# Rows of h stored as f16 pairs, transposed by DMA instead of by TensorE and ScalarE

## The chip, the cores and the metric

The kernel runs on 1 core of a Trainium2 chip (trn2). The metric is the device time of one launch in microseconds (us), the median of the runs; lower is better. PE is TensorE, DVE is VectorE, ACT is ScalarE, POOL is GpSimd and SP is SyncE, which only issues DMAs here.

## The reference

Two layers over x of 16 sequences x 512 positions x 256 features (8192 tokens), all in f32:

```python
# layer 0: causal attention with 16-wide q and k, values are x itself; layernorm; ternary-weight linear
q, k = x @ w_q.T + b_q, x @ w_k.T + b_k
x1 = softmax(where(causal, q @ k.T / 4, -1e4)) @ x          # added to x, normalised
x2 = layernorm(...) ; x2 @ (ternary(weight) * scale).T      # added, normalised
# layer 1: q, k, v = x @ qkv_w; a similarity of q and k per position gives one gate per position
#          (two small convolutions, softmax over the 512 positions); out = gate * v * ch_w @ proj_w
x3 = x2 + out_of_gate ; h = layernorm(x3) * ln_gamma + ln_beta
# experts: router logits h @ router_w.T, the best of 8 experts, plus one shared expert
shared = silu(h @ q(shared_w1).T) @ q(shared_w2).T           # 256 -> 512 -> 256, weights ternary per row
routed = gate * (silu(h @ q(expert_w1[e]).T) @ q(expert_w2[e]).T)   # for the token's expert e
out = layernorm(h + shared + routed)                         # written at the token's own row
```

What matters here is h, the normalised row of 256 numbers of each token. It is wanted in two layouts and twice: with the features on the partitions (transposed) as the operand of the router and of the shared expert, and again, gathered by expert, as the operand of the routed experts. Each time it is a pair of f16 numbers, a high part and a low part, so that four f16 matmuls stand for one in f32.

## The kernel before

The work has two stages that overlap around 500 to 600 us of the profile.

**The front** goes over the 16 sequences ("batches", b), one after the other, with several in flight: attention (proj, score, scoreT, pv), the ternary linear (x1T, ffn), the gate of layer 1 (x2T, dqk, fuse, u, the small ODE steps on DVE), and then for batch b the part that is changed:
`power2` (POOL, L4017) gives 1/sigma; `hn` (ACT, L1701) writes the normalised row to `HN` in f32, four calls of 128 x 256; `hT` (PE, L855) transposes HN into PSUM banks 6 and 7, two calls of four 128 x 128 transposes; `HT_` (ACT, L1712) evicts each bank as the f16 high part and `HTl_` (DVE, L2407) forms the f16 low part, both times scaled by ln_gamma (`gamc`, one number per partition); `logits` (PE, L865) and `up` (PE, L889) read `HT`; `router` and `place` (DVE) choose the expert and the row; `hsc` (POOL, L4043) scatters the rows of HN and `rsc` (POOL, L4052) those of the residual plus shared expert, `R`, by indirect DMA to two tables in HBM, `hrec` and `rrec`, sorted by expert. The token's number stands in the last column of HN (`hid`, L4034).

**The routed groups** take 256 rows of the tables each: w = 0 to 24 are whole groups of one expert, w = 25 to 35 are pairs of half groups of 128 rows, which may belong to two experts. Groups 0 to 13 can start when 12 batches are in the tables, the others after the last batch has been sorted. Per group: `gload` and `rload` (SP) fetch 256 rows of hrec and rrec; `gTr` (PE, L1060) transposes with four 128 x 128 transposes into one PSUM bank; `gT` (ACT, L1814) and `gTl` (DVE, L3045) evict high and low part to `G_T`; `gup` (PE, L1095), `gsilu` (ACT, L1845), `gSh` (ACT, L1859), `gSl` (DVE, L3053), `gdown` (PE, L1112), `gy` and `gx` (DVE, add bias and residual), `gbn` and `gve` (DVE), `gpower` (POOL, L4106), `gnb_` (DVE), `gn` (ACT, L1866), and two `scatter` (POOL, L4113) to the output rows; `gid_` (POOL, L4099) copies the token numbers out of the loaded rows.

The order of every engine is written out by hand, call by call: each engine is a list of such calls, with loops over pairs of batches (`for g in range(...)`) and over the groups from w = 18 on. An engine takes its list in order, so a call that waits holds up all behind it; SP too, whose list holds the loads of x and xT, of the expert weights, the small `maxima` DMAs (L493, the row maxima of the scores laid into one row, for which `scoreT` waits), and the group loads. Every call opens with its semaphore waits.

## Time and profile before

| | us |
|---|---|
| median of 3 runs (lowest, highest) | 792.61 (790.55, 793.23) |
| span of the profiled execution, first to last instruction | 794.0 |

| engine | busy us | share of the span | instructions |
|---|---|---|---|
| PE | 721.3 | 91% | 5417 |
| DVE | 699.8 | 88% | 2124 |
| ACT | 656.5 | 83% | 1447 |
| POOL | 335.0 | 42% | 370 |

No other time is given for the profiled execution than its span, so the span stands for its own time; it is 1.4 us above the median of the runs. Busy is the time in which an engine has at least one instruction under way, shared out among those that overlap, so the busy time of a group divided by its count is what one of them takes of the engine; its "mean ns" is from start to end and longer. The mean granted TensorE clock is 0.975 of full speed. Of the span, the front holds the first 550 us, with PE busy in nearly all of it; in the rest no engine is busy throughout.

### The profile page before, as it was taken

How to read it: one execution, taken by the hardware profiler on the slowest of the kernel's cores; microseconds unless marked ns; L12 is line 12 of the kernel's file. 1: busy time of each engine (PE TensorE's matmuls, PEld its weight loads, DVE VectorE, ACT ScalarE, POOL GpSimd, SP SyncE). 2: the span in 40 equal slices, each digit the busy share in tenths (PEclk: the TensorE clock that was granted, in tenths of full speed). 3: DMA queues.
4: the chain of work that ended last, by engine and by line, in shares of the span. 5: the costliest groups of instructions: out<-in, count | busy, mean ns of one | idle time of the engine just before them, and what ended most of it. 6: DMA issues, size and time to landing. Idle time of an engine off the chain costs nothing.

```text
span 794.0 us, 18530 instructions
## 1 busy us (share of the span) xinstructions
PE 721.3 (91%) x5417; PEld 546.5 (69%) x5417; DVE 699.8 (88%) x2124; ACT 656.5 (83%) x1447; POOL 335.0 (42%) x370
## 2 busy tenths in 40 slices
PE   3769998999999999999999999999989977988882
PEld 2556686777767767776776777777777766777771
DVE  5767888899989999998999999999899988998885
ACT  2265759997997998799799789988899976999994
POOL 3000011124334343342523335354567775876667
PEclk9979999999999999999999999999999998999996
DMA  8104301123132131213223023021624447455430
GB/s 264 35 15 119 106 2 55 34 90 98 55 107 70 55 129 43 80 61 108 87 61 114 29 80 108 14 88 41 211 71 149 145 152 206 147 177 163 136 119 30
DMA packets 57217, 76.51 MB, mean 96 GB/s; under 512 B 15453, under 2 KB 37919, under 8 KB 57120
## 3 DMA queue, kind: packets, MB, share of 16 engines
q1 hardware_dynamic: 46016, 48.45, 21.5%
q0 software_dynamic: 9600, 25.25, 8.9%
q10 hardware_dynamic: 1504, 1.64, 0.6%
q8 instruction: 46, 0.75, 0.4%
q14 instruction: 51, 0.42, 0.2%
HBM read 47.42 MB, written 28.91 MB: 96 GB/s over the span
## 4 chain that ended last, share of the span: by engine, by line
PE 67%; DVE 9%; ACT 8%; issue 7%; POOL 3%; DMA 3%; SPq 1%; ACTq 1%; DVEq 0%; POOLq 0%
PE bank L677 9%; PE bank L902 6%; PE bank L889 5%; PE bank L758 4%; PE bank L770 4%; PE bank L626 3%; PE bank L760 3%; PE bank L759 3%; ACT G_S L1845 3%; PE bank L1112 2%; POOL out L4113 2%; PE bank L705 2%; PE bank L716 2%; PE bank L706 2%; PE bank L855 2%
## 5 line engine op out<-in xcount | busy, mean ns | idle before, releaser
L4008 POOL TENSOR_TENSOR R<-rstd,mhalf 128x4 f32<-128x4 f32 x16 | 19.2, 1199 | 261.8 <-DVE rstd L2268 261.8
L4113 POOL DMA_INDIRECT out<-G_y,Gid x72 | 81.7, 1135 | 45.6 <-ACT G_y L1866 24.6
L1845 ACT ACTIVATE G_S<-bank,e1b,e1s 128x256 f32<-128x256 f32 (+1 forms) x188 | 87.1, 580 | 5.9 <-PE bank L1095 5.8
L1112 PE MATMUL bank<-E2T,split 128*128 x576 | 74.6, 284 | 14.5 <-DVE split L3053 11.9
L677 PE MATMUL bank<-X,PT 128*128 128x257 f32 x320 | 83.5, 401 | 0.5 <-ACT PT L1574 0.4
L1095 PE MATMUL bank<-G_T,E1T 128*128 128x256 f16 (+1 forms) x752 | 75.6, 251 | 7.8 <-issue 6.4
L4052 POOL DMA_INDIRECT rrec<-R,pos x64 | 67.8, 1060 | 30.7 <-issue 22.5
L1112 PEld LDWEIGHTS bank<-E2T,split 128*128 128x128 f16 x576 | 56.5, 101 | 27.4 <-issue 18.4
L4043 POOL DMA_INDIRECT hrec<-HN,pos x64 | 67.1, 1049 | 16.7 <-issue 15.9
L1095 PEld LDWEIGHTS bank<-G_T,E1T 128*128 x752 | 60.5, 99 | 17.9 <-issue 10.7
L677 PEld LDWEIGHTS bank<-X,PT 128*128 128x128 f32 x320 | 60.1, 200 | 10.5 <-issue 1.4
L889 PE MATMUL bank<-HT,E1T 128*128 128x512 f16 x240 | 60.3, 379 | 0.1
L4017 POOL TENSOR_TENSOR R<-V,mhalf 128x8 f32<-128x8 f32 x16 | 32.7, 2046 | 64.7 <-DVE V L2278 64.7
L902 PE MATMUL bank<-E2T,Sh 128*128 128x256 f16 x256 | 57.5, 273 | 0.8 <-DVE Sl L2448 0.8
L902 PE MATMUL bank<-E2T,Sl 128*128 128x256 f16 x256 | 57.4, 273 | 0.0
L3053 DVE SCALAR_TENSOR_TENSOR split<-G_S,sdn,split 128x1024 f16<-128x1024 f32 x36 | 47.0, 1306 | 9.1 <-ACT split L1859 9.1
L1866 ACT ACTIVATE G_y<-G_y,gnb,rstd 128x256 f32<-128x256 f32 x72 | 46.8, 661 | 7.5 <-DVE gnb L3038 7.5
L1726 ACT ACTIVATE S<-bank,e1b,e1s 128x512 f32<-128x512 f32 x64 | 49.2, 776 | 0.8 <-PE bank L889 0.4
L758 PE MATMUL bank<-WCh,TTh 128*128 128x512 f16 x128 | 48.7, 380 | 0.0
L760 PE MATMUL bank<-WCh,TTl 128*128 128x512 f16 x128 | 48.5, 379 | 0.0
L759 PE MATMUL bank<-WCl,TTh 128*128 128x512 f16 x128 | 48.5, 379 | 0.0
L2448 DVE SCALAR_TENSOR_TENSOR Sl<-S,sdn,Sh 128x512 f16<-128x512 f32 x64 | 47.1, 741 | 0.7 <-ACT Sh L1735 0.6
(438 smaller groups left out, 2292.8 us busy)
## 6 DMA issues: line engine op xcount, KB each, us to landing
...
G_h<-hrec SPq DMA_DIRECT2D x22, 128.5 KB, 2.4
G_r<-rrec SPq DMA_DIRECT2D x22, 128.5 KB, 2.5
```

The source lines that it names most:

```text
L677: last = pe.matmul(bk[:, 0:D + 1], PT[b % 2][:, o:o + P], X[b % 2][:, k, :], start=k == 0, stop=k == i)
L758: pe.matmul(bk[:], TTh[:, c, o], WCh[:, c, :], start=c == 0, stop=False)
L759: pe.matmul(bk[:], TTh[:, c, o], WCl[:, c, :], start=False, stop=False)
L760: last = pe.matmul(bk[:], TTl[:, c, o], WCh[:, c, :], start=False, stop=c == DC - 1)
L889: last = pe.matmul(banks[(7, 6)[f % 2]][:], E1T[:, NE, c, f * P:(f + 1) * P], ht(b)[:, x, c, :], start=k == 0, stop=k == 3)
L902: last = pe.matmul(out, x[:, f, j * P:(j + 1) * P], E2T[:, NE, f, :], start=k == 0, stop=k == 2 * FC - 1)
L1095: last = pe.matmul(bk[:, o + a:o + b], E1T[:, e, c, ff * P:(ff + 1) * P], gt[:, x, c, a:b], start=k == 0, stop=k == 3)
L1112: last = pe.matmul(down_bank(w)[:, j * D:(j + 1) * D], x[w % NGB][:, f, j * P:(j + 1) * P], E2T[:, expert_of[w, j], f, :], start=k == 0, s ...
L1845: last = act.activation(G_S[w % NGS][:, ff, a:b], bk[:, o + a:o + b], ACT.Silu, bias=e1b[:, e, ff], scale=e1s[:, e, ff])
L4043: pool.indirect_dma_start(hrec[:], bass.IndirectOffsetOnAxis(pos[b % 2][:, j:j + 1], 0), HN[b % 2][:, j, :], None).then_inc(s[f"hrec{b % 2 ...
L4052: pool.indirect_dma_start(rrec[:], bass.IndirectOffsetOnAxis(pos[b % 2][:, j:j + 1], 0), R[b % 2][:, j, :], None).then_inc(s[f"rrec{b % 2} ...
L4113: pool.indirect_dma_start(t["out"], bass.IndirectOffsetOnAxis(Gid[w % NGI][:, j:j + 1], 0), G_y[w % NGY][:, j, :], None, bounds_check=TOK ...
```

## The change

Three things are changed.

1. In the front DVE now writes the normalised row times ln_gamma in f32 (`hg`, four calls of 128 x 256, to a new tile HG), ACT copies all of it to f16 in one call (`hh`, 128 x 1024), and DVE subtracts to get the f16 low part (`hl`, 128 x 1024). HN holds both parts, 512 f16 numbers a row, and goes to hrec as it is. SP transposes it into HT with four transposing DMAs of 128 rows (`htr`). `hn`, `hT`, `HT_` and `HTl_` are gone. HT has two buffers instead of one.
2. A routed group's rows of hrec are transposed by the DMA that fetches them (`gload`), straight into G_T, which has 8 buffers instead of 4. `gTr`, `gT`, `gTl` and the tile G_h are gone. The PSUM banks that they used go to `gdown`, which has two banks at first and four later, instead of one and two. The token number moves from HN to the last column of R (258 columns now), and rrec is read with rows p and p + 128 on a partition instead of rows 2p and 2p + 1.
3. The lists of calls of all five engines are written anew. At the start SP now issues both weight loads of the shared expert (e2n, e1n) before xT(0) and x(0).

```diff
-HREC, RREC = D + 1, D + 1
+HREC, RREC = 2 * D, D + 2
...
-NGR, NGB, NGS, NGY, NGI = 5, 4, 3, 4, 8
+NGR, NGH, NGB, NGS, NGY, NGI = 5, 8, 4, 3, 4, 8
...
-    HT = sb("HT", [P, 2, DC, SEQ], F16)
-    HN = ring("HN", 2, [P, NT, HREC])
+    HT = [sb("HT0", [P, 2, DC, SEQ], F16)]
+    HN = ring("HN", 2, [P, NT, 2, D], F16)
...
+    HT.append(sb("HT1", [P, 2, DC, SEQ], F16))
+    HG = sb("HG", [P, NT, D])
...
-    def tr_bank(w):
-        return banks[0 if w < NSINGLE or w % 2 == 0 else 6]
+    DOWN = [(2, 0)[w % 2] if w < NSINGLE else (7, 6, 2, 0)[(w - NSINGLE) % 4] for w in range(NG)]
-        return banks[2 if w < NSINGLE or w % 2 == 0 else 7]
+        return banks[DOWN[w]]
-        if w < NSINGLE or w % 2 == 0:
-            return w - 1 if w <= NSINGLE else w - 2
-        return w - 2 if w - 2 >= NSINGLE else -1
-    def gathered(w):
-        return sum(16 if v < NF else 16 * NGT for v in range(w % NGR, w + 1, NGR))
+        return max([v for v in range(w) if DOWN[v] == DOWN[w]], default=-1)
+    def landed(w, n):
+        return sum(16 if v < NF else 16 * NGT for v in range(w % n, w + 1, n))
...
+        def htr(b):
+            if not 0 <= b < B:
+                return
+            sp.wait_ge(s["hl"], at("hl", b))
+            if b >= 2:
+                sp.wait_ge(s["up"], at("up", b - 2, 3))
+            for j in range(NT):
+                sp.dma_start_transpose(HT[b % 2][:].rearrange("p x c n -> p (x c) n")[:, :, j * P:(j + 1) * P],
+                                       HN[b % 2][:, j].rearrange("p x d -> p (x d)")).then_inc(s[f"hTd{b % 2}"], 16)
...
-            if w >= NGR:
-                sp.wait_ge(s["gTr"], at("gTr", w - NGR))
-                sp.wait_ge(s["gid"], w - NGR + 1)
+            if w >= NGH:
+                sp.wait_ge(s["gup"], at("gup", w - NGH, FC - 1))
             if w < NF:
                 o = sp.value_load(q_offi[0:1, w:w + 1], min_val=0, max_val=NE * CAP)
                 row_of[w] = o
-                sp.dma_start(G_h[w % NGR][:], hrec[bass.DynSlice(o, SLOT), :].rearrange("(p j) c -> p j c", p=P)).then_inc(s[f"gath{w % NGR}"], 16)
+                sp.dma_start_transpose(G_T[w % NGH][:].rearrange("p x c n -> p (x c) n"), hrec[bass.DynSlice(o, SLOT), :]).then_inc(s[f"gath{w % NGH}"], 16)
             else:
                 for j in range(NGT):
                     o = sp.value_load(m_offi[0:1, half(w, j):half(w, j) + 1], min_val=0, max_val=NE * CAP)
                     row_of[w, j] = o
-                    sp.dma_start(G_h[w % NGR][:, j, :], hrec[bass.DynSlice(o, P), :]).then_inc(s[f"gath{w % NGR}"], 16)
+                    sp.dma_start_transpose(G_T[w % NGH][:].rearrange("p x c n -> p (x c) n")[:, :, j * P:(j + 1) * P], hrec[bass.DynSlice(o, P), :]).then_inc(s[f"gath{w % NGH}"], 16)
 
         def rload(w):
...
-                sp.dma_start(G_r[w % NGR][:], rrec[bass.DynSlice(row_of[w], SLOT), :].rearrange("(p j) c -> p j c", p=P)).then_inc(s[f"gatr{w % NGR}"], 16)
+                sp.dma_start(G_r[w % NGR][:], rrec[bass.DynSlice(row_of[w], SLOT), :].rearrange("(j p) c -> p j c", p=P)).then_inc(s[f"gatr{w % NGR}"], 16)
...
-            pe.wait_ge(s["hn"], at("hn", b, 3))
-            for j in range(NT):
-                last = pe.transpose(banks[6 + k][:, j * P:(j + 1) * P], HN[b % 2][:, j, k * P:(k + 1) * P], ident[:])
-            last.then_inc(s["hT"], 1)
...
+            pe.wait_ge(s[f"hTd{b % 2}"], 16 * NT * (b // 2 + 1))
...
-            pe.wait_ge(s["HTl"], at("HTl", b, 1))
...
-                    last = pe.transpose(tr_bank(w)[:, o:o + P], G_h[w % NGR][:, j, c * P:(c + 1) * P], ident[:])
-            last.then_inc(s["gTr"], 1)
...
-                pe.wait_ge(s["gTl"], at("gTl", w))
+                pe.wait_ge(s[f"gath{w % NGH}"], landed(w, NGH))
...
-        def hn(b, j):
-            if j == 0:
-                act.wait_ge(s["rs2"], b + 1)
-                if b >= 2:
-                    act.wait_ge(s[f"hrec{b % 2}"], 16 * NT * (b // 2))
-                    act.wait_ge(s["hT"], at("hT", b - 2, 1))
-                if b < 2:
-                    act.wait_ge(s["guard"], 10)
-            act.activation(HN[b % 2][:, j, 0:D], X2[b % NX2][:, j, :], ACT.Copy, scale=R3[b % 4][:, 0, j:j + 1]).then_inc(s["hn"], 1)
-        def HT_(b, k):
-            act.wait_ge(s["hT"], at("hT", b, k))
-            if b == B - 1:
-                act.wait_ge(s["guard"], 20)
-            elif b >= 1 and k == 0:
-                act.wait_ge(s["up"], at("up", b - 1, 3))
-                act.wait_ge(s["logits"], at("logits", b - 1))
-            act.activation(ht(b)[:, 0, k, :], banks[6 + k][:], ACT.Copy, scale=gamc[:, k:k + 1]).then_inc(s["HT"], 1)
+        def hh(b):
+            if not 0 <= b < B:
+                return
+            act.wait_ge(s["hg"], at("hg", b, 3))
+            if b >= 2:
+                act.wait_ge(s[f"hrec{b % 2}"], 16 * NT * (b // 2))
+                act.wait_ge(s[f"hTd{b % 2}"], 16 * NT * (b // 2))
+            else:
+                act.wait_ge(s["guard"], 10)
+            act.activation(HN[b % 2][:, :, 0, :], HG[:], ACT.Copy).then_inc(s["hh"], 1)
...
-                act.wait_ge(s["gup"], at("gup", w - NGB, FC - 1))
-            for c in range(DC):
-                last = act.activation(G_T[w % NGB][:, 0, c, :], tr_bank(w)[:, c * SLOT:(c + 1) * SLOT], ACT.Copy, scale=gamc[:, c:c + 1])
...
-        def HTl_(b, k):
-            dve.wait_ge(s["HT"], at("HT", b, k))
-            dve.scalar_tensor_tensor(ht(b)[:, 1, k, :], banks[6 + k][:], gamc[:, k:k + 1], ht(b)[:, 0, k, :], ALU.mult,
-                                     ALU.subtract).then_inc(s["HTl"], 1)
+        def hg(b, j):
+            if not 0 <= b < B:
+                return
+            if j == 0:
+                dve.wait_ge(s["rs2"], b + 1)
+                if b >= 1:
+                    dve.wait_ge(s["hl"], at("hl", b - 1))
+            dve.scalar_tensor_tensor(HG[:, j, :], X2[b % NX2][:, j, :], R3[b % 4][:, 0, j:j + 1], gamr[:], ALU.mult, ALU.mult).then_inc(s["hg"], 1)
+        def hl(b):
+            if not 0 <= b < B:
+                return
+            dve.wait_ge(s["hh"], at("hh", b))
+            dve.tensor_tensor(HN[b % 2][:, :, 1, :], HG[:], HN[b % 2][:, :, 0, :], ALU.subtract).then_inc(s["hl"], 1)
...
-            dve.wait_ge(s["gT"], at("gT", w))
-            for c in range(DC):
-                last = dve.scalar_tensor_tensor(G_T[w % NGB][:, 1, c, :], tr_bank(w)[:, c * SLOT:(c + 1) * SLOT], gamc[:, c:c + 1],
-                                                G_T[w % NGB][:, 0, c, :], ALU.mult, ALU.subtract)
-            last.then_inc(s["gTl"], 1)
...
+                pool.wait_ge(s["zero"], 32 * NGT)
+            pool.iota(R[b % 2][:, :, D + 1].bitcast(I32), pattern=[[P, NT]], base=b * SEQ, channel_multiplier=1).then_inc(s["hid"], 1)
...
-            pool.indirect_dma_start(hrec[:], bass.IndirectOffsetOnAxis(pos[b % 2][:, j:j + 1], 0), HN[b % 2][:, j, :], None).then_inc(s[f"hrec{b % 2}"], 16)
+                pool.wait_ge(s["hl"], at("hl", b))
+            pool.indirect_dma_start(hrec[:], bass.IndirectOffsetOnAxis(pos[b % 2][:, j:j + 1], 0),
...
-            pool.tensor_copy(Gid[w % NGI][:], G_h[w % NGR][:, :, D].bitcast(I32)).then_inc(s["gid"], 1)
+            pool.tensor_copy(Gid[w % NGI][:], G_r[w % NGR][:, :, D + 1].bitcast(I32)).then_inc(s["gid"], 1)
...
```

On SP, in the front, between two loads of expert weights. Before (HN, HT, XT, X are tiles, NM the row maxima):

```order
L458 DMA e2n<-in_ew 128x2x512
L437 DMA XT<-in_xT 128x2x512
L493 DMA Qs<-NM_115 1x128x1 x4
L449 DMA e1n<-in_ew 128x4x256
L437 DMA XT<-in_xT 128x2x512
L430 DMA X_236<-in_x 128x4x256
```

and now:

```order
L462 DMA e2n<-in_ew 128x2x512
L426 DMA_TRANSPOSE HT_209<-HN_210 128x4x128 x4
L497 DMA Qs<-NM_115 1x128x1 x4
L453 DMA e1n<-in_ew 128x4x256
L441 DMA XT<-in_xT 128x2x512
L434 DMA X_235<-in_x 128x4x256
L426 DMA_TRANSPOSE HT_276<-HN_211 128x4x128 x4
L441 DMA XT<-in_xT 128x2x512
```

Per pair of batches eight transposing DMAs are new in SP's list, four ahead of the `maxima` DMAs of the even batch and four ahead of an xT load.

On PE, in the front, around the router's matmuls of an odd batch. Before (L855 is hT, L689 x1T, L626 proj, L865 logits):

```order
L855 MATMUL bank<-ident,HN_211 128x128 x4
L737 MATMUL bank<-R_149,cw_71 128x1 x2
L855 MATMUL bank<-ident,HN_211 128x128 x4
L689 MATMUL bank<-ident,X_237 128x128 x4
L626 MATMUL bank<-XT,wqk 128x512 x2
L865 MATMUL bank<-RW_88,HT 128x24 x16
```

and now (L781 is dqk, L710 x1T, L876 logits, L900 up, L661 score):

```order
L781 MATMUL bank<-WCh,TTl 128x512
L710 MATMUL bank<-ident,X_236 128x128 x4
L876 MATMUL bank<-RW_88,HT_276 128x24 x16
L900 MATMUL bank<-HT_276,E1T 128x512 x4
L661 MATMUL bank<-Ks,Qs 128x128
```

The transposes are gone, and logits now wait for the DMAs; the first matmuls of the shared expert follow at once.

On DVE, in the front, around the new calls of an even batch (L2210 and L2211 are qklo, L2336 hg, L2342 hl, L2253 T1l_, L2290 qks, L2220 max_):

```order
L2211 SCALAR_TENSOR_TENSOR Ks<-bank,bqk,Ks 32x512
L2336 SCALAR_TENSOR_TENSOR HG<-X_202,R_137,gamr 128x256
L2290 BN_STATS QS_151<-bank 128x6
L2696 RECIPROCAL esr<-esc 128x4
L2305 TENSOR_SCALAR CHW<-CHW 128x2
L2220 TENSOR_REDUCE NM_115<-bank 128x1 x2
L2342 TENSOR_TENSOR HN_210<-HG,HN_210 128x4x256
L2308 RECIPROCAL CHW<-CHW 128x2
L2253 TENSOR_TENSOR T1l<-bank,T1h 128x512
```

The list before had, ahead of the same call T1l_ (there L2327), only the low parts of both PSUM banks (L2407 is HTl_, L2373 to L2376 chw):

```order
L2728 TENSOR_SCALAR esc<-esc 128x4
L2373 TENSOR_TENSOR CHW<-bank,cb_72 128x2
L2731 RECIPROCAL esr<-esc 128x4
L2407 SCALAR_TENSOR_TENSOR HT<-bank,gamc,HT 128x512 x2
L2327 TENSOR_TENSOR T1l<-bank,T1h 128x512
L2376 TENSOR_SCALAR CHW<-CHW 128x2
```

DVE gives up two calls per batch there and takes five, the last of which waits for ACT.

## Rows read from the trace of the kernel before

**Rows 1.** Busy us of each engine in stretches; then PE clock, DMA share, GB/s.

```profile
192.00:512.00 320.00, 319.00 (x2277) 235.12 (x2275) 296.62 (x914) 281.62 (x633) 117.32 (x110) 1.00 0.24 76
560.00:670.00 110.00, 96.44 (x782) 77.03 (x783) 101.85 (x322) 96.48 (x189) 74.96 (x80) 0.94 0.50 152
680.00:700.00 20.00, 17.98 (x158) 15.11 (x159) 19.58 (x49) 20.00 (x42) 16.29 (x18) 1.00 0.59 182
722.00:780.00 58.00, 45.47 (x537) 39.40 (x534) 48.31 (x125) 57.92 (x135) 38.56 (x44) 1.00 0.42 127
```

**Rows 2.** Issues of xT in 150 to 520: duration, first and last start.

```profile
L437 SPq DMA_DIRECT2D XT<-in_xT x10: 367/374/374, 158.1 to 457.7; - x10
```

**Rows 3.** POOL in order of time, routed groups: start, duration, instruction, idle before.

```profile
676.50 1.50 POOL L4113 DMA_INDIRECT out<-G_y,Gid  x1 [0.23 <-DMA out<-G_y,Gid]
...
681.06 1.45 POOL L4113 DMA_INDIRECT out<-G_y,Gid  x1 [0.28 <-issue]
682.51 0.20 POOL L4099 COPY Gid<-G_h 128x2 int32<-128x2 int32 x1
683.18 0.98 POOL L4113 DMA_INDIRECT out<-G_y,Gid  x1 [0.46 <-issue]
684.15 1.17 POOL L4106 TENSOR_TENSOR rstd<-rstd,mhalf 128x2 f32<-128x2 f32 x1
...
745.48 1.20 POOL L4113 DMA_INDIRECT out<-G_y,Gid  x1 [0.71 <-DMA out<-G_y,Gid]
...
748.08 0.98 POOL L4113 DMA_INDIRECT out<-G_y,Gid  x1 [1.19 <-ACT G_y L1866]
...
751.00 1.20 POOL L4113 DMA_INDIRECT out<-G_y,Gid  x1 [0.71 <-DMA out<-G_y,Gid]
...
781.67 1.05 POOL L4113 DMA_INDIRECT out<-G_y,Gid  x1 [0.20 <-issue]
```

**Rows 4.** PE in order of time, early routed groups.

```profile
663.12 1.09 PE L1060 MATMUL bank<-ident,G_h 128*128 128x128 f32 x4 [3.68 <-DVE G_T L3045]
```

**Rows 5.** Instruction groups of PE: busy us, mean ns, idle before and releaser.

```profile
L1060 PE MATMUL bank<-ident,G_h 128*128 128x128 f32 x144 | 22.2, 279 | 8.3 <-DVE G_T L3045 4.2 <-DMA G_h<-hrec 4.0
L855 PE MATMUL bank<-ident,HN 128*128 128x128 f32 x128 | 19.9, 281 | 1.1 <-ACT HN L1701 1.1
```

**Rows 6.** The same view, groups of ACT.

```profile
L1859 ACT ACTIVATE split<-G_S,sdn 128x1024 f16<-128x1024 f32 x36 | 43.8, 1216 | 0.2
L1814 ACT ACTIVATE G_T<-bank,gamc 128x256 f16<-128x256 f32 x72 | 31.8, 522 | 6.7 <-PE bank L1060 6.6
L1701 ACT ACTIVATE HN<-X,R 128x256 f32<-128x256 f32 x64 | 28.7, 502 | 0.1
L1712 ACT ACTIVATE HT<-bank,gamc 128x512 f16<-128x512 f32 x30 | 20.3, 685 | 3.6 <-PE bank L855 2.7
```

**Rows 7.** The same view, groups of DVE.

```profile
L3045 DVE SCALAR_TENSOR_TENSOR G_T<-bank,gamc,G_T 128x256 f16<-128x256 f32 x72 | 30.8, 469 | 2.2 <-ACT G_T L1814 2.1
L2401 DVE SCALAR_TENSOR_TENSOR X<-U,WT,X 128x256 f32<-128x256 f32 x64 | 29.2, 473 | 0.0
L2407 DVE SCALAR_TENSOR_TENSOR HT<-bank,gamc,HT 128x512 f16<-128x512 f32 x30 | 21.6, 744 | 2.0 <-ACT HT L1712 1.5
L2349 DVE TENSOR_TENSOR X<-X,pb_row 128x1024 f32<-128x1024 f32 x16 | 19.4, 1210 | 0.0
```

**Rows 8.** The start, in order of time: start, duration, instruction.

```profile
1.25 0.46 SPq L437 DMA_DIRECT2D XT<-in_xT  x1
8.07 3.75 PE L626 MATMUL bank<-XT,wqk 128*128 128x512 f32 x4 [8.07 <-DVE bqk L2978]
```

**Rows 9.** DMA issues, KB each, us to landing; then SP's queue in 600 to 794.

```profile
G_h<-hrec SPq DMA_DIRECT2D x22, 128.5 KB, 2.4
Qs<-NM SPq DMA_DIRECT2D x48, 0.5 KB, 1.9
...
q1 hardware_dynamic: 13824, 17.38, 33.7%
```

1872 lines of the change are left out of this document (923 added, 949 removed), and 2 rows, old and new, of the table names.

## The prediction

> **What bounds the kernel now.** I read the stretches first, then the issues of xT for the period, then POOL in order of time in the routed groups, then the groups of instructions.
>
> In 192 to 512 us, the front in its steady state, PE is busy 319.0 of 320 us, DVE 296.6 and ACT 281.6 [rows 1]. Ten xT loads are issued from 158.1 to 457.7 us [rows 2], so a batch takes (457.7 - 158.1) / 9 = 33.3 us, and the 320 us are 9.6 batches. Per batch that is 33.2 us of PE, 30.9 of DVE and 29.3 of ACT. PE sets the pace of the front, and DVE has 2.4 us a batch to spare.
>
> In the routed groups no single engine does. In 680 to 700 us ACT is busy all the time, DVE 19.58 of 20 and PE 17.98 [rows 1], but POOL turns at the same pace: its first scatter of a group starts at 676.50 and again at 681.06, every 4.56 us, and between its calls there is only "issue" [rows 3]. The four calls and their gaps add up: 1.45 + 0.20 + 0.46 + 0.98 + 1.17 + 0.28 = 4.54 us. So POOL is full there though its busy share is 0.81. In the pairs of half groups, 722 to 780 us, ACT is busy 57.92 of 58 and the others 38 to 48 [rows 1]. POOL's period is 751.00 - 745.48 = 5.52 us, and now it waits for ACT's G_y (1.19 us) [rows 3]. ACT alone is the bound of the pairs. In 560 to 670 us, groups 0 to 11 with the last two batches between, DVE has 101.85 of 110 us, and PE stands still in places for the one transpose bank, as before the 3.68 us of the row at 663.12 [rows 1, 4].
>
> **The change, part by part.**
>
> PE loses 128 transposes of HN, 19.9 us, or 1.24 us a batch, and 144 of G_h, 22.2 us, or 0.62 us a group, and gets nothing [rows 5].
>
> ACT loses hn (28.7 us for 64) and HT (32 of 0.685, 21.9 us), together 3.16 us a batch, and gets hh, one call of 128 x 1024 from SBUF to f16. The nearest row is the same shape with a scale, 1.216 us [rows 6]. Net -1.95 us a batch. Per group it loses gT, 31.8 / 36 = 0.88 us [rows 6].
>
> DVE loses HTl, 2 x 0.72 = 1.44 us of the engine a batch (21.6 us for 30), and gets four hg: row L2401 is the same operation on 128 x 256 in SBUF, 0.473 us, so 1.89 us; and hl, one tensor_tensor of 128 x 1024, 1.21 us by L2349 [rows 7]. Net +1.66 us a batch. Per group it loses gTl, 30.8 / 36 = 0.86 us [rows 7].
>
> The front: demand per batch becomes PE 33.2 - 1.24 = 32.0, DVE 30.9 + 1.66 = 32.6, ACT 27.4 us. The bound passes from PE to DVE, with only 0.7 us below the present 33.3. DVE also waits for others now and then, as its 2.4 us of idle time shows, though most of that is waiting out PE. I give it 0.4 us of idle and get 33.0, -0.3 us a batch, -4 us over the 12 batches of the steady loop. The ends: no idle, 32.6, -8 us; all of its present idle kept, 35.0, +20 us.
>
> The new chain of a batch is hg, hh, hl, four DMAs, logits. What hides it: between hl and the first router call on DVE stand T1l, a qks, two max, four y and an x3, ten calls of 0.47 to 0.7 us by shapes like those of the DVE groups, some 6 us, and PE has score, fuse, ffn and scoreT to do meanwhile. A plain 128 KB load from hrec lands after 2.4 us [rows 9]; four with some 0.5 us of issue each would need about 4 us. That fits, so I price the chain at nothing. If cover is missing PE waits at logits, and the whole list of PE with it. On SP the four transposes stand ahead of the maxima DMAs (0.5 KB, 1.9 us to landing [rows 9]), for which scoreT waits; before, an xT load of 512 KB stood there, as many bytes.
>
> The start: xT(0) was issued at 1.25 us and proj(0) began at 8.07, held by the weights' scaling [rows 8]. Two loads of 512 KB now go ahead; at the plain load's 3.76 us per MB [rows 9] their 1.05 MB are 3.9 us, of which I take about half for slack. +1.5 us, ends 0 and +4.
>
> Groups 0 to 11, 560 to 670 us. DVE: 101.85 - 12 x 0.86 + 2 x 1.66 = 94.8; ACT: 96.5 - 12 x 0.88 - 2 x 1.95 = 82; PE: 96.4 - 12 x 0.62 - 2 x 1.24 = 86.5. With the 8.1 us that DVE is idle now it is 103, -7 us; the waits for the transpose bank go too, since PE reads what the DMA wrote, and gdown has a second bank. -8 us, ends -2 and -14. POOL, busy 75 us with some 0.3 us of gap after each of 60 DMAs, needs 93 and does not bind.
>
> Groups 12 to 35. From 676.50 to 781.67 [rows 3] there are 21 periods in 105.2 us. ACT would need 4.56 - 0.88 = 3.7 us in whole groups and 5.52 - 0.88 = 4.6 in pairs. POOL keeps all its calls, 4.56 us. So whole groups stay where they are, the pairs come down to about 4.6: 21 x 4.56 = 95.8, -9.4 us. The other end: if POOL's own calls get shorter beside a less busy DVE, whole groups go to 3.7 and pairs to 4.6, 10 x 3.7 + 11 x 4.6 = 88, -17 us. The last three groups drain as now.
>
> DMA: hrec's rows have 1024 bytes instead of 1028, so the bytes stay. New are 0.5 MB a batch from SBUF to SBUF, where the DMA share is 0.24 [rows 1]. What a transposing DMA takes no row shows. The nearest is the plain load: SP's queue moved 17.38 MB in 33.7% of 194 us [rows 9], 3.76 us per MB of all 16 engines, so 1.0 us for a group's 0.26 MB. I take a transposing load at that. In groups the share is 0.59 of 4.56 us = 2.7 us [rows 1]; 1.9 us are free, so it may cost 2.9 times the plain one before DMA is the bound.
>
> The Trainium skill is of two minds here. "Advanced Engine Details and Errata", X-Bar Transpose (TRN2), has transposing DMAs as fast as regular ones, which is what the sum does. "VectorE: DVE Perf Modes", The three transpose paths, gives 1309 ns to one 128 x 128 piece by DMA; a group has eight, and if they came one after the other that would be an estimated 10.5 us a group, over twice its period. No row here shows either.
>
> **Sum.** 794.0 - 4 + 1.5 - 8 - 9.4 = 774 us of span. The span lies 1.4 us above the median of the runs, so I predict 773.
>
> **Rivals.**
>
> A. The freed engines help more: DVE in the front at 32.7 (-7), groups 0 to 11 at -12, groups 12 to 35 at -17, start 0: 794 - 36 - 1.4 = 757. For it: three of the four engines get lighter in the tail, and POOL's own calls (1.45 and 0.98 us for the same scatter [rows 3]) look as if they took longer beside others' work. Against: the front's two engines both stand within 4% of the period.
>
> B. The front doesn't pay but costs: DVE, now the bound, keeps half of its idle time, 32.6 + 1.2 = 33.8, +0.5 x 12 = +6. The rest as forecast: 783. It is an engine that becomes the bound.
>
> C. The transposing DMAs are slow. This is the case on the other side. Its place is gload and htr, and it decides from 2.9 times the plain load's DMA time. At four times, a group needs 1.7 + 4.0 = 5.7 us of DMA: 21 x 5.7 = 120 against 105, +15; groups 0 to 11 gain nothing; in the front the four loads land about 2 us after PE wants them in half of the batches, +12. 794 + 27 + 1.5 - 1.4 = 821. At 3 times a group needs 4.7 us, 21 x 4.7 - 105 = -6.5, and with the late landing in the front: 794 - 6.5 + 12 + 1.5 - 1.4 = 800. For it: no row of such a DMA, and a second page that says so (above). Against: G_T has eight buffers, and logits stand some 6 us behind hl.
>
> D. The removed work was hidden and nothing is won: 792 to 793. Against: ACT is full in the pairs, and no other engine is.
>
> **Chances.** The forecast, 765 to 780: 0.48. A: 0.14. B, with what lies between it and no change: 0.14. D: 0.06. C in both sizes, with a front that keeps all its idle time (794 + 20 + 1.5 - 17.4 - 1.4 = 797): 0.18. A difference of 0.3%, 2.4 us, is about what can be told from none. So faster 0.76, the same 0.06, slower 0.18. The range that leaves out the fast end of A and most of C is 756 to 800; the forecast's own is 765 to 780.
>
> **What would show it.** Right: xT issues about 33.0 us apart, with DVE busy over 98% of the front and PE at 96%; POOL's scatters in the pairs 4.6 us apart with "issue" and no wait for G_y; hg at 0.47 and hl at 1.2 us; no wait of PE at logits or gup for a DMA. Wrong: the period of xT above 33.5, waits of logits for HT or of gup for G_T, a DMA share near 0.9 in the groups, transposes that hold SP for over 1 us each so that scoreT waits for the maxima. If POOL's period in whole groups falls well below 4.56, the gain is larger than forecast (A).

## The result: 8.6% slower, and the profile after

The changed kernel takes 859.71 us (857.95 to 862.27, 4 runs) against 791.58 (788.57 to 793.23, 4 runs) of the kernel before on the same chip: a ratio of 1.0855, interval 1.0817 to 1.0893. The forecast was 773 us. The profiled execution has a span of 856.9 us, 62.9 above that of before. Some executions of a kernel come out more than 1.5% above its fastest; the ratios leave these out, but the medians of runs 2, 5 and 12 hold one each, and the profiled execution of run 5 is one.

In the changed kernel's profile PE, DVE and ACT are not busier than before, they stand idle for longer. The first part of its page:

```profile
PE 719.1 (84%) x5145; PEld 527.1 (62%) x5145; DVE 693.3 (81%) x2100; ACT 604.2 (71%) x1297; POOL 348.7 (41%) x370
```

**Where the 62.9 us lie.** The issues of xT that I had used for the period [rows 2] are at other places of SP's new list, so that ten of them no longer stand for the same work (in the kernel with one transposing DMA they give 36.4 us a batch, where the work says 34.4). A better mark is DVE's first router call (r_lg), once per batch. For each kernel its row from the view of one line, batches 1 to 11 (duration of the call in ns, min/median/max, then first and last start in us). Before:

```profile
L2419 DVE TENSOR_REDUCE r_lg<-bank x11: 257/258/258, 158.7 to 495.3; 128x32 f32<-128x96 f32 x11
```

After:

```profile
L2353 DVE TENSOR_REDUCE r_lg<-bank x11: 256/257/258, 167.8 to 549.2; 128x32 f32<-128x96 f32 x11
```

(495.3 - 158.7) / 10 = 33.66 us a batch before, (549.2 - 167.8) / 10 = 38.14 after. So 9.1 us lie ahead of batch 1, 44.8 in the ten batches, and 307.7 - 298.7 = 9.0 behind batch 11.

Busy time in stretches. First the ten batches before:

```profile
158.70:495.30 336.60, 335.61 (x2381) 247.35 (x2380) 311.88 (x966) 293.64 (x666) 125.04 (x115) 1.00 0.26 81
```

After (the first answers to 192 to 512 us of [rows 1], the second is the ten batches, the third is in the late groups):

```profile
192.00:512.00 320.00, 290.38 (x1925) 206.59 (x1924) 274.12 (x831) 229.92 (x513) 103.54 (x98) 0.95 0.30 84
...
167.80:549.20 381.40, 344.19 (x2301) 246.46 (x2300) 324.72 (x995) 274.58 (x615) 119.94 (x113) 0.96 0.30 83
...
770.00:830.00 60.00, 49.31 (x549) 41.50 (x550) 46.75 (x117) 56.52 (x124) 55.51 (x50) 1.00 0.64 159
```

DVE needs 32.5 us a batch, near the forecast 32.6, and has 38.1. In 320 us PE, busy 319 before, is busy 290, at a granted clock of 0.95 instead of 1.00. What they wait for in the ten batches (us in total, times, longest), PE first, then DVE:

```profile
PE bank L684 <- DMA Qs<-NM: 20.4, 5, 5.1
PE bank L876 <- DMA HT<-HN: 12.0, 5, 3.2
...
DVE r_lg L2353 <- PE bank L876: 31.9, 10, 5.5
DVE X L2264 <- PE bank L727: 9.9, 5, 2.5
```

L684 is scoreT, which waits for the row maxima; L876 is logits. The chain of work that ended last, in order of time, leads there:

```profile
353.93 0.48 DVE HG L2336
...
355.80 1.15 DVE HN L2342
356.96 1.22 SPq L426
358.22 1.26 SPq L426
359.52 1.27 SPq L426
360.83 1.27 SPq L426
362.15 0.59 SPq L497
...
364.07 2.02 DMA Qs<-NM
366.13 0.79 PE bank L684
```

DVE ends the low part (hl), SP issues the four transposing DMAs, each of which holds its queue for 1.2 to 1.3 us, and only then the row maxima, of which DVE had finished the first two by 355.80 and the other two by 359.86, so that SP sends all four without a pause. The rows of these DMAs (duration of the issue in ns, min/median/max, then first and last start): HT of a batch, then G_T of whole groups (256 x 512) and of half groups (128 x 512):

```profile
L426 SPq DMA_TRANSPOSE HT<-HN x64: 1190/1267/2505, 128.1 to 658.1; - x64
...
L558 SPq DMA_TRANSPOSE G_T<-hrec x25: 1233/1262/2671, 615.5 to 760.0; - x25
...
L563 SPq DMA_TRANSPOSE G_T<-hrec x22: 1194/1213/1864, 763.1 to 815.5; - x22
```

**The late groups.** The power of POOL opens each group's normalisation. Its row for groups 18 to 33, before:

```profile
L4106 POOL TENSOR_TENSOR rstd<-rstd,mhalf x16: 1166/1235/1238, 702.4 to 780.2; 128x2 f32<-128x2 f32 x16
```

After:

```profile
L4067 POOL TENSOR_TENSOR rstd<-rstd,mhalf x16: 737/746/755, 771.5 to 843.8; 128x2 f32<-128x2 f32 x16
```

5.19 us a group became 4.82, in whole groups and pairs alike, where before it was 4.56 and 5.52 [rows 3]. One period after, in order of time:

```profile
796.48 0.69 DVE L2946 TENSOR_TENSOR G_y<-G_y,G_r 128x512 f32<-128x512 f32 x1
796.56 1.53 POOL L4074 DMA_INDIRECT out<-G_y,Gid  x1 [0.19 <-issue]
...
798.11 0.20 POOL L4060 COPY Gid<-G_r 128x2 int32<-128x2 int32 x1
...
798.22 0.16 DVE L2966 TENSOR_TENSOR rstd<-mv,G_r 128x2 f32<-128x2 f32 x1
...
798.29 1.28 DVE L2978 SCALAR_TENSOR_TENSOR split<-G_S,sdn,split 128x1024 f16<-128x1024 f32 x1
798.47 1.96 POOL L4074 DMA_INDIRECT out<-G_y,Gid  x1 [0.16 <-POOL Gid L4060]
...
800.44 0.74 POOL L4067 TENSOR_TENSOR rstd<-rstd,mhalf 128x2 f32<-128x2 f32 x1
```

A scatter of POOL writes 128 output rows, and DVE's split forms the f16 low part (gSl), reading two tensors of 128 x 1024 in SBUF. The scatter that took 0.98 us [rows 3] takes 1.96 and the power 0.74 instead of 1.17; with the gaps between them the four calls fill the 4.82 us. Before, DVE's split came 0.27 us behind the start of that scatter (683.18 [rows 3]):

```profile
683.45 1.28 DVE L3053 SCALAR_TENSOR_TENSOR split<-G_S,sdn,split 128x1024 f16<-128x1024 f32 x1
```

Now that gTl is gone from ahead of it, the split comes 0.18 us before the scatter.

### The profile page after: what moved, and what is told of

The parts are those of the page before. It is cut to its first block, busy times and chain, and to the rows that moved or that the text cites. A ratio compares the mean times of both kernels' runs of the same rounds, so it can differ in the third digit from the quotient of the medians.

```text
span 856.9 us, 17816 instructions
## 1 busy us (share of the span) xinstructions
PE 719.1 (84%) x5145; PEld 527.1 (62%) x5145; DVE 693.3 (81%) x2100; ACT 604.2 (71%) x1297; POOL 348.7 (41%) x370
## 4 chain that ended last, share of the span: by engine, by line
DVE 21%; issue 21%; PE 21%; POOL 14%; SPq 10%; DMA 8%; ACT 3%; POOLq 0%; DVEq 0%; ACTq 0%
SPq L426 8%; POOL out L4074 5%; PE bank L900 4%; DMA HT<-HN 4%; PE bank L698 3%; POOL rstd L4067 3%; DVE HG L2336 3%; DVE Sl L2382 2%; DVE HN L2342 2%; POOL rrec L4013 2%; POOL hrec L4002 2%; DVE bst L2247 2%; DMA Qs<-NM 1%; DMA e2n<-in_ew 1%; PE bank L684 1%
## 5 line engine op out<-in xcount | busy, mean ns | idle before, releaser
L4074 POOL DMA_INDIRECT out<-G_y,Gid x72 | 107.3, 1491 | 16.7 <-issue 9.8
L4002 POOL DMA_INDIRECT hrec<-HN,pos x64 | 70.6, 1103 | 59.7 <-DVE pos L2531 45.4
L1790 ACT ACTIVATE G_S<-bank,e1b,e1s 128x256 f32<-128x256 f32 (+1 forms) x188 | 80.4, 510 | 8.4 <-PE bank L1092 6.6
L900 PE MATMUL bank<-HT,E1T 128*128 128x512 f16 x256 | 71.0, 410 | 2.1 <-DMA HT<-HN 1.7
L913 PE MATMUL bank<-E2T,Sh 128*128 128x256 f16 x256 | 63.0, 289 | 6.0 <-DVE Sl L2382 5.9
L1811 ACT ACTIVATE G_y<-G_y,gnb,rstd 128x256 f32<-128x256 f32 x72 | 41.6, 593 | 32.9 <-DVE gnb L2972 29.0
L913 PE MATMUL bank<-E2T,Sl 128*128 128x256 f16 x256 | 62.9, 289 | 0.0
L3976 POOL TENSOR_TENSOR R<-V,mhalf 128x8 f32<-128x8 f32 x16 | 27.5, 1721 | 86.0 <-DVE V L2204 86.0
L1541 ACT ACTIVATE PT<-bank 128x512 f32<-128x512 f32 (+1 forms) x64 | 26.6, 435 | 39.0 <-PE bank L685 38.4
L684 PE MATMUL bank<-Qs,Ks 128*128 128x512 f32 (+1 forms) x64 | 29.9, 499 | 24.3 <-DMA Qs<-NM 22.0
L781 PE MATMUL bank<-WCh,TTl 128*128 128x512 f16 x128 | 49.2, 384 | 0.0
```

The costliest lines, as they stand in the source:

```text
L900: last = pe.matmul(banks[(7, 6)[f % 2]][:], E1T[:, NE, c, f * P:(f + 1) * P], HT[b % 2][:, x, c, :], start=k == 0, stop=k == 3)
L913: last = pe.matmul(out, x[:, f, j * P:(j + 1) * P], E2T[:, NE, f, :], start=k == 0, stop=k == 2 * FC - 1)
L1790: last = act.activation(G_S[w % NGS][:, ff, a:b], bk[:, o + a:o + b], ACT.Silu, bias=e1b[:, e, ff], scale=e1s[:, e, ff])
L4002: pool.indirect_dma_start(hrec[:], bass.IndirectOffsetOnAxis(pos[b % 2][:, j:j + 1], 0), HN[b % 2][:, j].rearrange("p x d -> p (x d)"), No ...
L4074: pool.indirect_dma_start(t["out"], bass.IndirectOffsetOnAxis(Gid[w % NGI][:, j:j + 1], 0), G_y[w % NGY][:, j, :], None, bounds_check=TOK ...
```

## The experiments

The kernel before took 791 to 793 us on the chips of the runs 1 to 4 and 9 to 12, and 809 to 811 on those of the others, so a ratio is compared only within one group of four runs (17 and 18 are a group of two), and across groups the periods of the traces are used. These differ too: one and the same front, that of run 3, gave 34.41 and 34.43 us a batch (runs 3 and 9), 35.0 (run 6), and 34.71, 35.24 and 34.65 (runs 13, 14 and 16), so differences of some 0.6 us across groups show nothing. Nor does a ratio carry over: run 9, in effect run 3 again, has 1.02 where the kernel before takes 791 us, while run 5, which is run 3 with other group loads, has 1.00 where it takes 809. "Per batch" is always the mark above.

**Run 1, the start.** The expert weights' loads go behind xT(0) again.

```diff
-        load_e2(0)
-        load_e1(0)
         load_xT(0)
+        load_e2(0)
+        load_e1(0)
```

> The changed kernel (859.7 us) with one edit: xT(0) is issued first again, ahead of the two weight loads of the shared expert. In the changed kernel proj(0) started at 12.8 us against 8.1 before. Theory S (the start is late by the two loads ahead of it and the delay runs through to the end): 855, that is 4 to 5 us less. Rival (something else holds the start as well, or the front absorbs it): within 1.5 us of 859.7.

855.27 us, ratio 1.0813 (1.0754 to 1.0871): its interval overlaps that of the changed kernel. In the traces proj(0) starts at 8.07 us, as before the change, instead of 12.82, and the router call of batch 11 comes at 545.3 instead of 549.2. By these the start is worth 4 to 5 us, not 1.5.

**Run 2, the order on SP.** `maxima(2 * g)` ahead of `htr(2 * g - 4)`.

> The changed kernel with one edit on SP: in each pair of batches the four small maxima DMAs of the even batch are issued ahead of its four transposing DMAs, not behind them. Theory H (each transposing DMA holds SP's sequencer for 1.27 us, so four delay what is behind them by 5.1 us): scoreT waits 3.7 us a pair less for the maxima, logits of the even batch get HT about 2 us later: 840 to 852. Theory B (the transposing DMAs load the DMA engines, their order on SP does not matter): within 3 us of 859.7. Theory V (VectorE, which has 1.7 us more a batch, and the new order of calls set the front's pace): within 3 us of 859.7.

857.4 us, 1.0809 (1.0723 to 1.0895), 37.5 us a batch. A miss: the hold has only changed its victim. In the ten batches PE no longer waits for the row maxima, but 29.5 us for HT, where it was 12.0.

**Run 3, one transposing DMA a batch** instead of four. HT is laid out by blocks of 128 rows so that one DMA of 128 x 2048 can write it.

```diff
-            for j in range(NT):
-                sp.dma_start_transpose(HT[b % 2][:].rearrange("p x c n -> p (x c) n")[:, :, j * P:(j + 1) * P],
-                                       HN[b % 2][:, j].rearrange("p x d -> p (x d)"))
+            sp.dma_start_transpose(HT[b % 2][:].rearrange("p j x c n -> p (j x c) n"),
+                                   HN[b % 2][:].rearrange("p j x d -> p (j x d)"))
```

> The changed kernel with HT laid out by tile, so that one transposing DMA of 128 x 2048 takes the place of four of 128 x 512 per batch: the same bytes through the same transposing path. Theory H: if the hold is per instruction (a group's load of 256 x 512 holds SP as long as one of 128 x 512, 1.26 us), SP is free 3.8 us a batch earlier, HT and maxima come 3.8 us earlier, the period falls from 40.0 to about 35 us: 795 to 815. If the hold goes by the amount moved: 859. Theory B: the same bytes are transposed, no gain, 850 to 862. Theory V: no gain, 850 to 862.

806.67 us, 1.0193 (1.0139 to 1.0247): 53 us of the 68 are gone. The DMA's row, the mark, and PE's wait for the maxima:

```profile
L425 SPq DMA_TRANSPOSE HT<-HN x16: 1342/1982/3562, 129.0 to 609.6; - x16
...
L2352 DVE TENSOR_REDUCE r_lg<-bank x11: 257/258/258, 162.2 to 506.3; 128x32 f32<-128x96 f32 x11
...
PE bank L683 <- DMA Qs<-NM: 6.5, 5, 1.7
```

The hold is 2.0 us instead of 5.1, a batch takes 34.41 us, and the wait for the maxima is down from 20.4 to 6.5 us. The one DMA lands after 4.4 us.

**Run 4, four plain DMAs** of the same bytes, HT not transposed (so router and shared expert compute on other numbers).

> The changed kernel with the four transposing DMAs of HN to HT of each batch replaced by four plain DMAs of the same bytes (HT then is not transposed; the router sees other numbers). Theory H: a plain DMA holds SP about 0.45 us, so 1.8 us a batch in place of 5.1: 805 to 825. Theory B: the bytes go through without the transposing path, 795 to 815 as well, and then the last run tells. Theory V: no gain, 850 to 862.

803.04 us, 1.014 (1.0085 to 1.0196), 34.26 us a batch; the issue is held for 0.60 us:

```profile
L426 SPq DMA_DIRECT2D HT<-HN x64: 465/601/841, 130.6 to 604.8; - x64
```

On this one chip a batch takes 38.2 us with four transposing DMAs (run 1), 34.4 with one and 34.3 with four plain ones. The bytes are the same in all three, run 4 has the number of DMAs and run 3 the transposing of all bytes, and both are fast. So it is the four holds of the transposing form that make the front slow. From the router call of batch 11 to the power of group 12 the changed kernel takes 740.6 - 549.2 = 191.4 us, run 3 and run 15 take 185.4 and 185.1, run 4 takes 179.8, and the kernel before 675.0 - 495.3 = 179.7. Other runs with run 3's front take 183.3 to 186.6 us there, so the four holds cost the last batches some 6 us, and 12 by run 4.

**Run 5, plain DMAs in the groups** (from run 3; the experts compute on rows that are not transposed).

> The kernel with one transposing DMA a batch (806.7 us), and in the routed groups gload fetches the same 256 rows x 1024 bytes with a plain DMA, untransposed, so the experts compute on unsorted numbers (that part of the computation is changed). Theory D (the groups are slowed by the transposing DMAs: DMA share .87 in places, SP held 1.2 us for each of 58): groups 12 to 35 go from 4.82 us a group to below 4.56, the time to 790-798. Theory P (the groups' pace is POOL's own list, 4.82 us of scatters, power and copy, lengthened by DVE's work on two SBUF operands beside it): the period stays 4.82, and the time stays at 803-807, perhaps 1 to 3 us less around groups 0 to 11.

Ratio 0.9999 (0.9969 to 1.0028). The period of the late groups in its trace stays at 4.81 us (734.4 to 806.6 for 15). The transposing DMAs don't set the pace of the late groups.

**Run 6, POOL's scatter ahead of the token numbers** (from run 3).

> The kernel with one transposing DMA a batch (806.7 us); in POOL's loop from w = 18 on, scatter(w - 6, 0) stands ahead of gid(w - 5) instead of behind it, so that it starts some 0.36 us earlier, before DVE's split (L2977, 1.28 us) instead of 0.2 us into it. Theory P (a POOL call that starts while DVE has an operation on two SBUF operands under way stands until that ends): this scatter goes from 1.97 us to about 1.0, the period of a group from 4.82 to about 4.5, where ACT (56.5 of 60 us busy) takes over; 18 periods, so -4 to -6 us, 801-803. Rival (a scatter of that place takes 1.97 us for another reason, or the loop is set by DVE, ACT and PE): period 4.82 and 806-807.

1.0046 (1.0015 to 1.0076), period 4.93. A miss: POOL leaves 0.31 us between the two scatters, the second starts at 752.14 and the split at 752.03, so the scatter is still 0.11 us behind the split's start and takes 2.02.

**Run 7, all maxima first** (the edit of run 2 on run 3).

> The kernel with one transposing DMA a batch (806.7 us), and SP issues maxima(2g) ahead of htr(2g - 4). In the kernel with four transposing DMAs this order won nothing (857.4 against 859.7). Theory W (what the front still lacks, 34.4 against 33.65 us a batch before, is PE waiting at scoreT for the row maxima, 1.4 us per pair of batches, and DVE waiting behind it at r_lg and X): 34.4 goes to 33.6, the time to 798-800. Theory V (DVE's demand of 32.5 us a batch with its usual 2 us of idle time sets the period): another wait takes its place, 804-807.

1.0178 (1.0112 to 1.0244), 15 us above run 5 and 9 above run 6 by the medians; 35.7 us a batch against 35.0 of run 6, both of which have run 3's front. The wait changes its place:

```profile
PE bank L875 <- DMA HT<-HN: 10.5, 5, 2.3
```

**Run 8, less work a batch on DVE** (the projection bias is added on 32 of 256 columns; the rest is left out). DVE's busy time in the ten batches is 0.7 us a batch below that of run 6.

> The kernel with one transposing DMA a batch (806.7 us), and x2p, DVE's addition of the projection bias on 128 x 1024 (1.21 us a batch), is done on 128 x 128 of it (0.3 us or less), so 0.9 to 1.0 us a batch less of DVE; the rest of the bias is left out. Theory V (DVE sets the front's period): 34.4 goes to 33.4-33.6 us a batch, the time to 795-798. Theory W (the wait for the row maxima sets it) or PE's demand: at most -3 us, 803-807.

1.0118 (1.0058 to 1.0178), 35.45 us a batch against 35.0 in the same group: no gain, so DVE's demand is not what sets the front. That it comes out slower than runs 5 and 6 is not explained.

**Run 9, POOL's order of the kernel before** (from run 3).

> The kernel with one transposing DMA a batch, POOL's loop from w = 18 on in the order of the kernel before: gpower(w - 5), scatter(w - 6, 0), gid(w - 5), scatter(w - 6, 1) instead of gid, scatter, gpower, scatter. Theory P (a POOL call beside a DVE operation on two SBUF operands stands until that ends; DVE's split of 1.28 us comes right behind gve): now the power stands beside the split and takes about 1.2 us instead of 0.74, and the scatter behind it starts when the split is over and takes 1.0 to 1.5 instead of 1.97; the period of a late group goes from 4.82 to 4.5-4.6, 15 to 18 periods, -4 to -5 us. It also lets gnb come sooner behind gve. Rival: the period stays at 4.82 whatever the order (DVE, ACT and PE set it).

1.0213 (1.0162 to 1.0264), period 4.81. It says nothing on the theory: taken around the loop, scatter, power, scatter and copy alternate as they did, and each meets the same DVE call.

**Runs 10 and 11, the hold by itself in the kernel before.** Four more DMAs a batch into a tile that nobody reads, transposing in run 10 and plain in run 11.

```diff
+            for j in range(NT):
+                sp.dma_start_transpose(DUM[:, j].rearrange("p (a n) -> p a n", n=P), E1T[:, NE, 0, :])
...
+            extra(g)
             load_xT(2 * g)
...
+            extra(g)
             maxima(2 * g)
```

> The kernel before (792 us) with nothing changed but four more transposing DMAs (128 x 512 f16, SBUF to SBUF, into a tile that nobody reads) a batch on SP's queue in batches 5 to 14: four ahead of load_xT(2g), four ahead of maxima(2g). Theory H (each holds SP's list for 1.27 us): 5.1 us a batch, the row maxima late behind them; if before's list has no slack the pair of batches takes 3 to 6 us more over 5 pairs, 805-820. Rival (the four DMAs are harmless, and the changed kernel's 4 us a batch come from its order and its DVE work): 792-796.

> As the run before, but the four are plain DMAs of the same 128 x 512 f16 numbers from and to the same tiles, some 0.5 us of SP each. Theory H: 2 us a batch, hidden for the greater part: 792-797, and clearly under the transposing ones. Rival (any four DMAs cost the same, by their bytes): the same time as the transposing ones.

791.45 us, 1.002 (0.999 to 1.005), and 790.23 us, 1.000 (0.9969 to 1.0031). The forecast of theory H fell, though the hold is there:

```profile
L521 SPq DMA_TRANSPOSE DUM<-E1T x40: 1194/1270/2257, 138.4 to 459.3; - x40
...
L2433 DVE TENSOR_REDUCE r_lg<-bank x11: 257/258/258, 156.0 to 492.6; 128x32 f32<-128x96 f32 x11
```

33.66 us a batch, to the hundredth as before. These DMAs wait for nothing that comes late, so SP takes them while it would be idle: in the pair of batches at 320 us the four end at 326.07, and the maxima go out from 327.54. In the changed kernel SP may start only when hl is done, and two of the maxima are then already due. The hold costs time only between an event that comes late and a reader that waits.

**Run 12, ACT issues the transposing DMA** of batches 0 to 11 (from run 3).

> The kernel with one transposing DMA a batch, for batches 0 to 11 issued by ACT (behind PS(2g + 2) and gexp(2g + 3)) instead of SP, so that SP's list has nothing ahead of the row maxima. The hold of 2.0 us moves to ACT, which is busy 27.3 of 34.4 us a batch. Theory W (what is left in the front is SP's list: the wait of scoreT for the row maxima): PE's wait at L683 for Qs<-NM goes, 34.4 to 33.7 us a batch, -6 to -8 us against the run with SP. Theory O (the order of DVE's list makes the maxima late whatever SP does, and ACT's hold delays T1h): no gain or up to +5 us.

1.0247 (1.0191 to 1.0303): by the medians 3 us above run 9, with overlapping intervals, so no gain. The trace has 35.16 us a batch, but its execution is 7 us above the median. PE's wait for the maxima falls to 1.5 us, and two others come:

```profile
PE bank L872 <- DMA HT<-HN: 5.1, 4, 1.9
PE bank L706 <- DVE T1l L2260: 3.6, 2, 2.2
```

By these rows ACT's list has no free place for 1.9 us either.

**Run 13, DVE's gy ahead of the split** in the groups of the loop from w = 18 on (from run 3).

> The kernel with one transposing DMA a batch (806.7 us); in DVE's loop from w = 18 on gy(w - 6), which reads PSUM, stands ahead of gSl(w - 5), the split, which reads two SBUF tensors for 1.28 us. So the split starts 0.7 us later, behind the start of POOL's scatter and not 0.2 us ahead of it. Theory P (a POOL call beside a DVE operation on two SBUF tensors stands until that ends): the scatter of 1.95 us takes about 1.0, the power behind it up to 1.2 instead of 0.74, and the period of a late group goes from 4.82 to 4.5-4.6 where ACT is full: -4 to -6 us. Rival (the period of 4.82 is a ring of DVE, ACT and PE, or the scatter takes that long anyway): 4.8 to 5.0 and no gain.

1.0098 (1.0055 to 1.014). The whole groups come to 4.4 to 4.5 us, the pairs rise to 5.1. POOL in a pair:

```profile
761.83 0.98 POOL L4073 DMA_INDIRECT out<-G_y,Gid  x1 [1.46 <-ACT G_y L1810]
762.80 0.76 POOL L4066 TENSOR_TENSOR rstd<-rstd,mhalf 128x2 f32<-128x2 f32 x1
763.75 1.05 POOL L4073 DMA_INDIRECT out<-G_y,Gid  x1 [0.18 <-issue]
```

Both scatters are short now, and POOL waits for ACT, which is busy 29.0 us of 760 to 790. DVE stands 1.3 us ahead of each gy; which of the other engines closes that ring of 5.1 us I have not resolved.

**Run 14, the split cut to 64 of 1024 columns** from w = 18 on (most of the low part is left out).

> The kernel with one transposing DMA a batch; from w = 18 on DVE's split is done on 64 of its 1024 columns (the rest of the low part is left out), some 0.15 us instead of 1.28. Theory P: the scatter behind the token numbers goes from 1.95 to 0.9-1.1 us and the period from 4.82 to 4.5-4.6 (ACT full) though nothing else on POOL is changed. Rival (the scatter takes 1.95 us for another reason): the scatter stays at 1.95 and the period at 4.8.

0.9973 (0.9947 to 0.9999). Whole groups take 3.8 to 3.9 us, pairs 4.8, with ACT busy 50.0 of 50 us there:

```profile
763.87 0.98 POOL L4073 DMA_INDIRECT out<-G_y,Gid  x1 [1.56 <-ACT G_y L1810]
...
765.80 1.05 POOL L4073 DMA_INDIRECT out<-G_y,Gid  x1 [0.18 <-issue]
...
740.00:790.00 50.00, 43.74 (x514) 36.82 (x513) 31.34 (x105) 50.00 (x115) 34.78 (x45) 1.00 0.66 167
```

The scatter of 1.96 us is 0.98 without any edit on POOL, and 0.99 in a whole group (at 745.03). Theory P holds, and ACT bounds the pairs. Runs 13 and 14 together show that the split beside the scatter made the whole groups' period.

**Run 15, the changed kernel without the transposing DMAs from HN to HT** for batches 2 to 15 (so router and shared expert read old rows); all else in the lists as it is.

> The changed kernel (859.7 us), in which only batches 0 and 1 have their transposing DMAs from HN to HT; the later batches use what stands in HT (router and shared expert of the other batches are computed on the wrong rows). All engines' lists stay as they are. It shows the front of the new lists without these DMAs at all. Theory H (the DMAs behind hl, their hold of SP and their landing, make the front slow): the period falls from 38.1 to at most 34.3 us a batch. If it comes down to 33.0 the forecast of the engines' demand was right, and the remaining 1.3 us of the one-DMA version are the DMA chain's too; if it stays at 34.0 to 34.4, these are the new lists' own (DVE's idle time that I had counted as hidden).

1.0002 (0.9975 to 1.0029). The ten batches:

```profile
L2353 DVE TENSOR_REDUCE r_lg<-bank x11: 245/257/259, 167.5 to 508.0; 128x32 f32<-128x96 f32 x11
...
167.50:508.00 340.50, 331.42 (x2303) 239.96 (x2302) 324.65 (x995) 271.96 (x615) 119.66 (x113) 1.00 0.24 77
```

34.05 us a batch against 38.14: 4.1 us are the DMAs', with the uncertainty of two chips; on one chip it was 3.9 from run 1 to run 4. The 0.4 us over the 33.66 of before may be the new lists', but that is less than the same front differs between chips, so it is not shown. The ratio of 1.0002 is from a chip where the kernel before takes 810 us and doesn't say that the DMAs cost all of the 8.6%. PE has 12.8 us less busy time for the same instructions, at a clock of 1.00 instead of 0.96.

**Runs 16 to 18, towards a best version.** Run 16 is run 3 with the edits of runs 1 and 13. Run 17 is the same with gy ahead of the split in whole groups only, and with the maxima around the DMA; run 18 is run 3 with that last edit alone:

```diff
-            htr(2 * g - 4)
-            maxima(2 * g)
+            maxima(2 * g, (0, 1))
+            htr(2 * g - 4)
+            maxima(2 * g, (2, 3))
```

> A try at the best version: one transposing DMA a batch, xT(0) ahead of the expert weights at the start, and gy ahead of the split in the late groups. 806.7 - 4 (start) - 5 (late groups, if theory P holds) = 798; still above the kernel before (792).

> The best version that the runs point to: one transposing DMA a batch, xT(0) ahead of the expert weights, in the late whole groups gy ahead of the split (the pairs keep the old order), and SP issues the first two row-maxima DMAs of an even batch ahead of the transposing DMA and the last two behind it. From 1.0006 of the kernel before: whole groups at 4.4 us and pairs at 4.82 -2 to -3 us, the row maxima -4 us (34.65 to 34.2 us a batch): a ratio of 0.991 to 0.995. If the swap of waits seen with all maxima first (PE then waits for HT) comes again, 1.000.

> The version with one transposing DMA a batch (1.0193), and only the row maxima of even batches in two halves around the transposing DMA. Theory W2 (scoreT waits because all four maxima DMAs stand behind 2.0 us of hold, though two of them are ready before it): PE's wait for Qs<-NM falls from 1.4 us a pair to under 0.3, the front from 34.4 to 34.1 us a batch, a ratio of 1.013 to 1.016. Rival (HT comes later by the two issues, 1.2 us, and PE waits there instead, as when all four went first): 1.018 to 1.022.

Run 16: 1.0006 (0.9981 to 1.0031). Run 18: 0.9965 (0.9947 to 0.9984), 34.35 us a batch, PE's wait for the maxima down to 0.6 us; run 3 itself was not run on that chip, so what this edit alone gains in time is open. Run 17: 803.17 us against 811.34, 0.9894 (0.9862 to 0.9926), with

```profile
L2353 DVE TENSOR_REDUCE r_lg<-bank x11: 242/256/258, 162.9 to 503.7; 128x32 f32<-128x96 f32 x11
...
332.93 1.58 SPq L496 DMA_DIRECT2D Qs<-NM  x2
334.61 1.91 SPq L425 DMA_TRANSPOSE HT<-HN  x1
337.20 1.12 SPq L496 DMA_DIRECT2D Qs<-NM  x2
```

34.08 us a batch, about what run 15 has with no DMA, and no wait of PE for Qs or HT stands in its list any more. It is 1.1% faster than the kernel before on that chip. Its profiled span is 801.6 us, only 4.0 below run 3's on a chip where the kernel before took 793 us and run 3 was 1.9% slower; whether run 17 beats the kernel before on such a chip was not run, and these figures don't suggest it.

## Why the prediction was wrong

**The step that failed** is the chain of a batch: "four with some 0.5 us of issue each would need about 4 us. That fits, so I price the chain at nothing", and with it SP's four transposes ahead of the maxima, priced at nothing as "as many bytes" as the xT load in their place. A transposing DMA holds SP for 1.27 us, four for 5.14, and the cover was not there: SP starts at hl's end (356.96), the maxima go out from 362.15, and scoreT and logits wait, 20.4 and 12.0 us in ten batches. Priced by what was measured, that is about +4 us a batch (run 15; runs 1 and 4), some 41 of the 62.9 us, and some 6 us more in the last batches. I had bounded the DMA's load on the 16 engines and not its hold on the queue, though I had named it, in the last paragraph, among the signs of being wrong; without a row for it, the bound should have been open upwards and rival C should have had its place on SP. C's mechanism, slow transposing transfers that fill the DMA engines in gload, did not come about: plain loads there change nothing (run 5). Its late landing in the front, about 2 us in half of the batches, is near what PE waits for HT (12.0 us, 5 times in ten batches), but what makes HT late is the hold: each DMA lands 2.5 us after its issue, against 2.1 for a plain one.

**The front's demand.** The base was off first: the xT issues gave 33.3 us a batch where the mark gives 33.66, so PE had 33.6 and DVE 31.2 us a batch, not 33.2 and 30.9. DVE at 32.6 then came out right (32.5) partly by luck, as its net addition is 1.3 us, not 1.66; hg, hh and hl take 0.48, 1.06 and 1.21 us each by their rows, near what was forecast. PE was to lose 1.24 us and to need 32.0; in run 15, at the same granted clock of 1.00, it went from 335.6 to 331.4 us in ten batches, 0.4 us a batch, and needs 33.1. The term was taken from a group's busy time, and that is more than what a group takes of PE, other than I said ahead of the prediction: the groups of PE in the ten batches before add up to 540.9 us where PE is busy 335.6. So the bound did not pass to DVE. Without the DMAs PE is busy 97% of the time and DVE 95%, and 0.7 us less DVE work gains nothing (run 8). DVE's idle time there is 34.05 - 32.5 = 1.6 us, not the 0.4 that I gave it; I had called the old idle time mostly "waiting out PE", but in the ten batches before, DVE's listed waits are 12.7 us for ACT and 6.7 for PE. Without the DMAs the front would have been about where it was or 0.4 us a batch slower, instead of 0.3 faster. That is near rival B's size (+0.5), but not its mechanism, in which DVE is the bound.

**The start** was to cost 1.5 us, ends 0 and 4; it costs 4 to 5 (run 1). The slack that I took for half of the two loads was not there: proj(0) waits for XT until 12.82 us.

**Groups 0 to 11** were to give 8 us. In the stretch from batch 11 to group 12, 180 to 185 us without the holds against 179.7 before, no gain is left, though PE, DVE and ACT got lighter (DVE from 165.5 to 156.4 us in run 4). DVE's waits there in run 4 name POOL, which I had said does not bind:

```profile
DVE gnb L2972 <- POOL rstd L4067: 8.1, 6, 3.6
DVE G_y L2935 <- DMA out<-G_y,Gid: 7.8, 5, 2.7
```

Before, the first of these was 1.3 us and the second is not in the list. POOL in turn waits there for DVE, and no run tests which of them sets this stretch, so its cause stays open.

**Groups 12 to 35** were to give 9.4 us. From the power of group 12 to that of group 33 it is 843.8 - 740.6 = 103.2 us against 780.2 - 675.0 = 105.2, -2.0. I took POOL at 4.56 us because it "keeps all its calls". It does, but their length hangs on what DVE does beside them: 4.82, whole groups and pairs. ACT's forecast for pairs, 4.6, is 4.8 in run 14. Rival A's thought that POOL's calls take longer beside others' work [rows 3] was right, with the sign turned: less DVE work moved the split onto the scatter.

The Trainium skill's rule in "Advanced Engine Details and Errata", X-Bar Transpose (TRN2), that transposing DMAs are as fast as regular ones, is not borne out where it matters here: they land in 2.5 us against 2.1 of plain ones (HT in the changed kernel and in run 4), but hold the queue for 1.27 against 0.60 us. The 1309 ns for one 128 x 128 piece of "VectorE: DVE Perf Modes", The three transpose paths, is near the hold of one instruction here, but that instruction moves four or eight such pieces.
